# Mixture-of-experts decoder layer: whole turns of eight blocks, then one half turn of four, in place of whole turns alone

## The reference

```python
x = layernorm(x + dilated_self_attention(x))
x = layernorm(x + cross_attention(x, ctx))
# mixture of experts: 32 experts, the best 8 for each token
w, sel = top_k(softmax(x @ gate_w), 8);  w = w / sum(w)
# each expert takes its tokens in order, 1024 at most:
y = (silu(xg @ w_gate[e]) * (xg @ w_up[e])) @ w_down[e]     # 256 -> 96 -> 256
x = layernorm(x + sum over the 8 experts of w * y)
```

## Time and profile before

| | us |
|---|---|
| median of 3 runs | 569.25 |
| lowest, highest | 568.72, 569.51 |
| profiled execution, its own time | 570.47 |
| profiled execution, span from first to last instruction | 568.6 |
| mean granted TensorE clock in the span | 0.953 |

### The profile page before, as it was taken

The page is one execution under the profiler, slowest core; times in us unless marked ns, Lnnn a source line. Parts: engine busy times, 40 slices in busy tenths (PEclk is TensorE's granted clock), DMA queues, the critical chain, the costliest instruction groups (busy, mean ns, idle before and its releaser), DMA issues.

```text
span 568.6 us, 16506 instructions
## 1 busy us (share of the span) xinstructions
PE 503.3 (89%) x4567; PEld 407.1 (72%) x4568; DVE 384.0 (68%) x1539; ACT 343.5 (60%) x1240; POOL 385.9 (68%) x596
## 2 busy tenths in 40 slices
PE   2789999999999999994179999999999999995894
PEld 2456666666666666652079999999999999994683
DVE  1258888888898889864336666666666666664874
ACT  2277777777777777782036666666666666660112
POOL 5534766776777777676718888888888878883533
PEclk9599999999999999998569999999999999997899
DMA  9299999999522222222346665666566656658995
GB/s 200 69 338 267 285 337 388 346 335 335 182 92 92 81 92 92 83 104 106 127 140 203 201 195 181 210 195 193 187 201 204 190 181 192 206 173 321 422 423 164
DMA packets 79835, 118.48 MB, mean 208 GB/s; under 512 B 12339, under 2 KB 69565, under 8 KB 77760
## 3 DMA queue, kind: packets, MB, share of 16 engines
q1 hardware_dynamic: 63456, 78.63, 45.8%
q0 software_dynamic: 13824, 37.78, 18.0%
q10 hardware_dynamic: 2528, 1.74, 1.0%
HBM read 56.07 MB, written 66.22 MB: 215 GB/s over the span
## 4 chain that ended last, share of the span: by engine, by line
PE 62%; DVE 10%; ACT 7%; DMA 7%; issue 7%; POOL 5%; SPq 0%; ACTq 0%; DVEq 0%; POOLq 0%
PE bank L816 18%; PE bank L832 12%; PE bank L808 7%; PE bank L621 6%; DMA wall<-results 5%; ACT pr L912 5%; PE bank L631 4%; POOL queues L549 3%; PE bank L677 3%; PE bank L826 3%; PE bank L615 2%; PE bank L701 1%; PE bank L703 1%; PE bank L639 1%; DVE nmax L1070 1%
## 5 line engine op out<-in xcount | busy, mean ns | idle before, releaser
L573 POOL DMA_INDIRECT results<-ys,wcol x152 | 150.1, 987 | 26.0 <-POOL pscrap L562 23.9
L549 POOL DMA_INDIRECT queues<-x,xidx x128 | 127.1, 993 | 41.4 <-issue 38.4
L816 PE MATMUL bank<-wall,xtT 128*128 x624 | 129.3, 330 | 0.1
L816 PEld LDWEIGHTS bank<-wall,xtT 128*128 128x128 f32 x624 | 99.4, 193 | 0.5 <-issue 0.5
L912 ACT ACTIVATE pr<-bank,nmax 128x128 f32<-128x128 f32 x256 | 90.1, 372 | 14.1 <-DVE nmax L1070 13.2
L832 PE MATMUL bank<-wall,hT 96*128 x304 | 90.8, 379 | 0.0
L1011 ACT ACTIVATE ys<-bank,wcol 128x256 f32<-128x256 f32 x152 | 71.9, 473 | 28.0 <-PE bank L832 28.0
L1282 DVE SCALAR_TENSOR_TENSOR tg<-th,bank 128x96 f32<-128x96 f32 x156 | 39.5, 253 | 54.8 <-ACT th L1005 54.7
L808 PEld LDWEIGHTS bank<-ident,xt 128*128 128x128 f32 x314 | 61.7, 197 | 19.9 <-DMA xt<-queues 12.2
L808 PE MATMUL bank<-ident,xt 128*128 128x128 f32 x314 | 62.6, 281 | 11.8 <-DMA xt<-queues 11.8
L621 PE MATMUL bank<-kP,qS 128*128 128x512 f32 x128 | 67.4, 609 | 0.3 <-DVE eAT L1108 0.3
(11 more groups left out here) (190 smaller groups left out, 902.0 us busy)
## 6 DMA issues: line engine op xcount, KB each, us to landing
xt<-queues SPq DMA_DIRECT2D x162, 160.0 KB
results<-zeros SPq DMA_DIRECT2D x16, 1024.0 KB
wall<-results SPq DMA_DIRECT2D x16, 1024.0 KB, 19.7
queues<-zeros SPq DMA_DIRECT2D x2, 1760.0 KB, 9.7
wall<-in_L_ffn_w_gate SPq DMA_DIRECT2D x4, 768.0 KB
wall<-in_L_ffn_w_up SPq DMA_DIRECT2D x4, 768.0 KB
wall<-in_L_ffn_w_down SPq DMA_DIRECT2D x4, 768.0 KB
results<-ys,wcol POOLq DMA_INDIRECT x152
```

The costliest lines, as they stand in the source:

```text
L549: pool.indirect_dma_start(xg, bass.IndirectOffsetOnAxis(ap=xidx[:, par, k:k + 1], axis=0), x2[:, par, :], None, bounds_check=last_row, oob ...
L573: pool.indirect_dma_start(yr, bass.IndirectOffsetOnAxis(ap=wcol[:, u, 1:2], axis=0), ys[:, u, :], None, bounds_check=last_y, oob_is_err=Fa ...
L816: ins = pe.matmul(bank[2 + u % 2][:, 0:2 * INTER].rearrange("p (g i) -> p g i", g=2), xtT[:, u % 2, kk, :], wall[:, bass.ds(e, GU)].rearrange(
```

## The change

The number of blocks is now rounded up to a multiple of four in place of eight. The tables give two numbers: `rounds`, which counts the values 4, 12, 20, ... below the number of blocks (at least 1), and `half`, which is the old count less `rounds`, so 0 or 1. Each engine reads both. After its loop over `rounds` turns it has a second loop over `half` turns with four blocks in its body. The final waits of DVE count one more load or scatter for the buffers that the half turn uses. For 145 to 148 blocks there are 18 whole turns and a half one; for 149 to 152 there are 19 whole turns and none.

```diff
-        tab_n = sb("tab_n", [1, 1], I32)
+        tab_n = sb("tab_n", [1, 2], I32)
...
 # SP (and likewise POOL, PE, ACT, DVE)
             rounds = sp.value_load(tab_n[0:1, 0:1], min_val=1, max_val=MAXB // UN)
+            half = sp.value_load(tab_n[0:1, 1:2], min_val=0, max_val=1)
...
-            with sp.Fori(0, rounds) as j:
+            def loads(j, n):
                 rows = rows_of(j * UN + 2 * UN)
-                for u in range(UN):
+                for u in range(n):
                     ...
+            with sp.Fori(0, rounds) as j:
+                loads(j, UN)
+            with sp.Fori(0, half):
+                loads(rounds, HALF)
...
 # POOL
+            with pool.Fori(0, rounds) as j:
+                results_out(j, UN)
+            with pool.Fori(0, half):
+                results_out(rounds, HALF)
...
 # PE, behind its loop
+            with pe.Fori(0, half):
+                for u in range(HALF):
+                    t = rounds * UN + u
+                    down(t, u, down_e[u])
+                    block_T(t + 5, u + 5, rounds)
+                    turn_h(t + 2, u + 2)
+                    gu(t + 4, u + 4, gate_e[u])
...
 # ACT
+            with act.Fori(0, rounds) as j:
+                blocks(j, UN)
+            with act.Fori(0, half):
+                blocks(rounds, HALF)
...
 # DVE, tables
-                dve.tensor_scalar(tjunk[:, :], blk[0:1, 0:MAXB:UN], pW[0:1, 130:131], 0.0, ALU.is_lt, ALU.add,
-                                  accum_out=rnds[:, :]).then_inc(s, 1)
+                dve.tensor_scalar(tjunk[:, 0, :], blk[0:1, 0:MAXB:UN], pW[0:1, 130:131], 0.0, ALU.is_lt, ALU.add,
+                                  accum_out=rnds[:, 0:1]).then_inc(s, 1)
+                dve.tensor_scalar(tjunk[:, 1, :], blk[0:1, HALF:MAXB:UN], pW[0:1, 130:131], 0.0, ALU.is_lt, ALU.add,
+                                  accum_out=rnds[:, 1:2]).then_inc(s, 1)
                 dve.wait_ge(s, H("n"))
-                dve.tensor_scalar(tab_n[0:1, :], rnds[:, :], 1.0, None, ALU.max).then_inc(s, 1)
+                dve.tensor_scalar(rnds[:, 2:3], rnds[:, 1:2], 1.0, None, ALU.max).then_inc(s, 1)
+                dve.wait_ge(s, H("full"))
+                dve.tensor_copy(tab_n[0:1, 0:1], rnds[:, 2:3]).then_inc(s, 1)
+                dve.tensor_tensor(tab_n[0:1, 1:2], rnds[:, 0:1], rnds[:, 2:3], ALU.subtract).then_inc(s, 1)
...
 # DVE, expert loop and the waits behind it
+            with dve.Fori(0, rounds) as j:
+                blocks(j, UN)
+            with dve.Fori(0, half):
+                blocks(rounds, HALF)
+            turns = dve.snap(rounds + half)
             for u in range(UN):
-                dve.wait_ge(xt_in[u], rounds * 16 + (32 if u < 2 else 16))
+                dve.wait_ge(xt_in[u], (turns if 2 <= u < 2 + HALF else rounds) * 16 + (32 if u < 2 else 16))
                 hold(2 + u)
             for u in range(UN):
-                dve.wait_ge(y_out[u], rounds * 16 + 16)
+                dve.wait_ge(y_out[u], (turns if u < HALF else rounds) * 16 + 16)
                 ins = hold(2 + UN + u)
```

More of the change, by code:

```diff
@@ L195, in build @@
         past = sb("past", [NE, TAB], BF16)
-        tjunk = sb("tjunk", [1, MAXB // UN])
-        rnds = sb("rnds", [1, 1])
+        tjunk = sb("tjunk", [1, 2, MAXB // UN])
+        rnds = sb("rnds", [1, 3])
         tab_g = sb("tab_g", [1, TAB + 2 * UN], I32)
@@ L246, in build @@
         peH = Steps(sem("peH"), "count place table back")
-        dveH = Steps(sem("dveH"), "took nblk nblkb skipb cum past n n2 short back1 back2 last reached fe fx tg tw ts twice tx")
+        dveH = Steps(sem("dveH"), "took nblk nblkb skipb cum past r8 n full n2 n3 short back1 back2 last reached fe fx tg tw ts twice tx")
         peF = {n: sem(f"peF_{n}") for n in ("xT", "gu", "hT", "y")}
@@ L567, in _, with results_out @@
             rounds = pool.value_load(tab_n[0:1, 0:1], min_val=1, max_val=MAXB // UN)
-            with pool.Fori(0, rounds) as j:
-                for u in range(UN):
+            half = pool.value_load(tab_n[0:1, 1:2], min_val=0, max_val=1)
+            def results_out(j, n):
+                for u in range(n):
                     pool.wait_ge(held, j * UN + (u + 1))
@@ L799, in _ @@
             rounds = pe.value_load(tab_n[0:1, 0:1], min_val=1, max_val=MAXB // UN)
+            half = pe.value_load(tab_n[0:1, 1:2], min_val=0, max_val=1)
             def block_T(t, u, j):
@@ L992, in _ @@
             rounds = act.value_load(tab_n[0:1, 0:1], min_val=1, max_val=MAXB // UN)
+            half = act.value_load(tab_n[0:1, 1:2], min_val=0, max_val=1)
             def block_T(t, u):
@@ L1020, in _, with blocks @@
                 tanh(t, t)
-            with act.Fori(0, rounds) as j:
-                for u in range(UN):
+            def blocks(j, n):
+                for u in range(n):
                     t = j * UN + u
@@ L1266, in _ @@
             rounds = dve.value_load(tab_n[0:1, 0:1], min_val=1, max_val=MAXB // UN)
+            half = dve.value_load(tab_n[0:1, 1:2], min_val=0, max_val=1)
             def weights(t, u, j, column):
@@ L1299, in _, with blocks @@
                 gate(t + 2, t + 2)
-            with dve.Fori(0, rounds) as j:
-                for u in range(UN):
+            def blocks(j, n):
+                for u in range(n):
                     t = j * UN + u
```

## The result

| | before | after |
|---|---|---|
| median (6 runs each), us | 569.76 | 563.87 |
| lowest, highest | 568.72, 571.02 | 563.32, 565.28 |
| profiled execution, own time | 570.47 | 563.56 |
| its span | 568.6 | 561.4 |

The ratio is 0.9901, with a 95% interval of 0.9886 to 0.9917: 5.6 us less (4.7 to 6.5); between the two medians lie 5.9. Forecast were 563.7 and a gain of 5.5. In a second comparison with the same kernel before the ratio was 0.9895 (0.9876 to 0.9914).

The account below looks back on a forecast made before the run. PE's pace was taken to bound the expert loop: four blocks at 1.425 us give 5.70, less 0.2 for the half turn's entry, 5.5 off 569.25, so 563.7 us, range 562.3 to 565.8.

Parts of the forecast that it names:

- What bounds the loop: Expert loop: PE, busy throughout, sets the pace alone; dropping four empty or padded blocks saves 5.70 us.
- The pace, 1.425: Expert loop: PE takes 1.425 us for each block, padded ones too, the mean of 1.42 and 1.43.
- sign for another pace: Expert loop after the change: a pace other than 1.425 us would mean that the loop body was moved.
- The landing: Loop's end: the last, empty scatter takes 2.12 us to land; a real one before it, 2.8, costs nothing.
- the 3.55 from which it would count: Loop's end: the last real scatter, issued 1.43 us before the empty one, may take 3.55 us before it ends the loop.
- The tables at nothing: Ahead of the loop: 0.55 us more table work, hidden beside the queues' scatters, for which SP waits 6.1 us; cost 0.
- The entry at 0.2: Change from whole turns to half turn: leaving one loop and entering another costs 0.2 us.
- Late code: Rival, half turn's entry: PE stands for instruction transfers, 2.0 us per large one; 565.5 us for one, 567.5 for two; chance 0.09.
- The slower rival: Whole turns: moved code must be fetched at each jump back; 570.8 us at 0.4 per turn, 599.6 at 2.0; chance 0.03.
- The reading back: Stage behind the loop: shifts whole, beginning about 508.1; as rival, PE's half clock costs up to 1.7 us, 565.5; chance 0.07.
- The range's high end, 565.8: Upper end of the forecast time, said to take in one large instruction fetch and the reading back at half clock.
- Nothing shortened from 149 blocks on: Rival, block count: with 149 or more, 19 turns run as before, 569.3 us, within 0.2%; chance 0.03.

Follow-up runs that it names:

- E4: Changed kernel with 18 whole turns and the half turn branched around, 144 blocks, three real blocks left out; 557.98 us, ratio 0.9790 to the kernel before.
- E1: The changed kernel run again without edit, 148 blocks, beside the kernel before; 563.35 us, ratio 0.9895.
- E9: Kernel before with only three small tiles (tjunk, rnds, tab_n) enlarged, moving later tiles 92 bytes; 569.02 us, ratio 0.9994 to the kernel before.
- E8: Changed kernel with a branch around the half turn in place of the loop over it; 563.46 us, ratio 0.9889 to the kernel before.
- E3: Changed kernel with three blocks in the half turn in place of four, 147 in all, all real; 562.24 us, ratio 0.9871 to the kernel before.
- E12: Changed kernel with two memsets on DVE ahead of the last step of the tables, delaying them; 563.83 us, ratio 0.9905 to the kernel before.
- E6: 18 whole turns, then a second loop running one whole turn of eight, 152 blocks as in the kernel before; 569.11 us, ratio 0.9984 to it.
- E7: Changed kernel with never-run code on PE, ACT and DVE between whole turns and half turn, jumped over; 569.63 us, ratio 1.0004 to the kernel before.
- E11: Changed kernel rewritten for any count: whole turns, then up to seven single blocks behind branches, here 147 blocks; 563.83 us, ratio 0.9903 to the kernel before.
- E10: Changed kernel with never-run code between whole turns and half turn on ACT and DVE alone; 563.91 us, ratio 0.9899 to the kernel before.
- E2: Changed kernel without the half turn's four unused loads, DVE waiting only for the whole turns' loads; 563.26 us, ratio 0.9881 to the kernel before.

## Why the prediction was right

- **What bounds the loop.** Right: four blocks at PE's pace were the gain. Three sizes (E4, E1, before) lie near one line, and the empty scatters had given the right number of blocks: after the change the last scatter still carries no data.
- **The pace, 1.425.** It was taken as one for both kernels. It is 1.4267 before and 1.4234 after, and E9 shows that tile sizes make the difference: about 0.5 us over the loop, a gain that no step had. The prediction's sign for another pace, a moved loop body, doesn't fit: E9 moved no code.
- **The landing.** An empty scatter was expected to end the loop, with 2.12 us to land. It took 2.12 again in the profile after, but a load of `xt` held DVE's waits, and the ending was 2.42 and 2.53 in two profiles (0.2 to 0.3 over before; 2.28 in E8). Loads were not among the things that could be late next. The estimate of 2.8 for a scatter with data, under the 3.55 from which it would count, came out with less room than it seemed: as the last one it took 2.58 (E3) and 2.43 (E4), but as the last but one 3.26 after the change and 3.53 in E12. That it cost nothing is right by a narrow margin.
- **The tables at nothing.** Right: after the change 4.8 us of cover were left, and E12 used 4.6 of them without loss.
- **The entry at 0.2.** Too high: nothing, by PE's timeline and E6. DVE has 0.47 us to spare there.
- **Late code.** It didn't happen, for the reason given, that the half turn is read straight on. The price was too low: up to 2.0 for one transfer, where E7 paid 3.53 of standing and 1.9 at the slow clock behind it.
- **The slower rival.** No instruction transfer in the whole turns after the change either, and the pace didn't rise.
- **The reading back.** 54.8 us in place of 55.0 in the profiles, though its half clock lay elsewhere: shifted as a whole. It begins at 506.6 in place of the 508.1 forecast, by the 1.05 us ahead of block 16 and the 0.45 of the pace. The range's high end, 565.8, holds one large fetch or a reading back at half clock (565.5 each), not both.
- **Nothing shortened from 149 blocks on.** Wrong as priced if the loop construct tests behind its body: the half turn would then run on top of 19 whole turns. No run has such inputs.

The sum of what was measured is 5.69 for four blocks and 0.5 for the pace, less 0.2 for the ending: 6.0, or 0.9895 of 569.76. Forecast were 5.5; measured were 0.9901 and 0.9895. The mechanism is the one forecast. That the number is so near owes something to luck: the entry, taken off and not paid, makes up for the longer ending, which the forecast did not have. What is left between 5.5 and 6.0 is the pace.

## What to carry to other kernels

In a loop bound by one engine, rounding up to whole turns costs that engine's pace for each empty block, and the bytes per scatter show how many are empty. A remainder placed straight behind the loop cost nothing at its entry here; the same code behind a long taken branch cost PE 3.5 us and then its clock, 5.4 in all. What ends a stage is a set of waits: take off the critical engine's work, and then look at when the last loads and scatters land and at the form of the last waits, which together took back all of one more block in E11.

## What the hardware showed unasked

- Enlarging three tiles by 92 bytes in all, with no other change, made a block 3.3 ns shorter, by the starts of PE's instructions wholly in the two transposes that read `xt` (229.9 to 226.7 ns for the pair).
- An instruction fetch behind a taken branch held PE for 3.53 us, though the 16 KB transfer within it took 0.9; DVE stood 0.70 at its own (E10). That stop of PE, in the midst of work at 2.4 GHz, was followed by 1.6 us at a mean granted clock of 0.68 and 3.4 us at 0.65.
- The same kind of scatter of 128 rows landed 2.1 to 2.6 us after its issue without data (before, E10) and 2.4 to 4.4 us after it with data (E2, E11), at the loop's end.
